# A graph layer in one launch: the second group of row sums, with ScalarE's high part ahead of the gate rows and an earlier reload of the partial sums

## The chip, the cores and the metric

The kernel runs on one core of a Trainium2 chip. The time is that of the device for one launch, in microseconds (us), and a kernel's time is the median of its runs.

## What is computed

The layer takes 1250 nodes with 1024 features and 20000 edges of 8 types. Cut to what matters here:

```python
xn = layernorm(x)
u = xn @ root + bias
for r in range(8):                       # relations
    mask = edge_type == r
    mean = segment_sum(xn[src] * mask, dst) / max(count, 1)
    u = u + mean @ weight[r]
z = concat([u, xn]) @ w_gate + b_gate
h = tanh(u) * z + xn * (1 - z)
x = x + h + linear_attention(xn)
x = x + fp4_ffn(layernorm(x))
```

## The kernel before, in words

The rows are cut into 10 tiles of 128 (NT). All products of the normalised x stand in one long run of TensorE: 21 column blocks (NH), each with 10 tiles, so 210 steps (NSTEP). Block 0 is the query, key and value projection, blocks 1 to 16 the eight relations with two halves each, 17 and 18 the root matrix, 19 and 20 the lower half of the gate matrix (from step 190, NT * H_GATE). Numbers are carried as a high part and a low part, so a step (`product`, L1877) is 24 matmuls of 128x512: high by high, high by low and low by high.

`xn[src] @ weight[r]` is taken as a product of all rows first; its results go to HBM (relation_rows), and the sums over edges are made by fetching rows of it. That is done in two groups of relations (0 to 4, then 5 to 7), tile by tile of the destination rows. For one tile of group two there are 7 items (`gather_items`, L133): places 0 and 3 are *left-over* items, places 1, 2, 4, 5 and 6 are *planes*. Ten tiles are spread over steps 178 to 207, so a tile takes three steps:

- step A: places 0, 1, 2; step B: places 3 and 4; step C: places 5 and 6.

Group two has the sums numbered 10 to 19 (`m.sum`). Each item is one fetched block of 128 rows of 1024 numbers, in a ring of 4 buffers (source_rows). GpSimd fetches item m + 4 as soon as item m has been used (`gather`, L940), with an indirect DMA.

A plane is one instruction of VectorE (`plane`, L1592, recorded at L1605): sum = rows * weight + sum, in u_sum0 or u_sum1 by the sum's parity. The first plane of a tile in group two reads the partial sum of group one, which SyncE has loaded back from HBM (`load_sum`, L696, recorded at L699).

A left-over item goes to TensorE. ScalarE makes its high part (`left_over_hi`, L2400, source_rows_hi, L2405), VectorE the one-hot (L1586) and the low part (`left_over`, L1583, source_rows_lo, L1589), and TensorE multiplies both by the one-hot at the end of the *next* step (`aggregate`, L2019, L2015, 4 matmuls). High and low part have one buffer each, so the next left-over item waits for these matmuls. After the low part of place 0 VectorE finishes the tile before (`finish`, L1609): it adds the matmuls' result (L1615) and the root rows (L1620), and SyncE stores the sum (`store_sum`, L701, L703) and loads the next root rows (`load_root`, L688, L694).

From step 190 on, VectorE empties a product's bank itself, since it adds the gate's bias (`evacuate_gate`, L1640, L1647), first thing in the step after the product. ScalarE only sends those rows out, with a DMA it issues after waiting for VectorE (`evacuate`, L2329, L2335). Before step 190 ScalarE empties the bank (L2345) and sends (L2347).

Each engine goes through the steps in its own program order:

- ScalarE (L2426): `evacuate(n - 1)`, `hi_row` (the high part of one 128x512 block of the weights to come, WH, L2317), `left_over_hi`;
- VectorE (L1652): `evacuate_gate(n - 1)`, then the step's items;
- GpSimd (L964): `low_rows` (L875, the low part WL of that block, L879), then the fetches;
- SyncE (L727): the load of the weight block four ahead (`load_raw`, L633, L642), which waits until an earlier block's low part is made, then for the items of the step: at place 2 `store_sum` and `load_root`, at place 5 `load_sum` for the next sum, which waits until the sum two before, from the same buffer, is stored (`stored_sum`, L518).

Of the kernel before, what the change touches and what calls it, by code (L numbers as in the profile page):

```python
# [22 lines left out]
NT = -(-N // P)  # L23
# [16 lines left out]
NBK = NG * NT  # L40
# [29 lines left out]
H_GATE = H_ROOT + 2  # L70
# [96 lines left out]
def gps_layer(nc, x, src, dst, edge_type_8, weight, root, bias, w_gate, b_gate, gamma, w_q, w_kv,  # L167
              w_out, ff_gate, ff_up, ff_down, out):
    with ExitStack() as ctx:
# [313 lines left out]
        def prod_bank(n):  # L483
            return 4 + n % 4
# [133 lines left out]
        def _(sp):  # L618
# [77 lines left out]
            def load_sum(rd, i):  # L696

                stored_sum(sp, rd, i - 2)
                sp.dma_start(ACCS[i % 2][:], u_d[rows(i % NT), :]).then_inc(sum_in[i % 2], 16)  # L699

            def store_sum(rd, i):  # L701
                sp.wait_ge(acc_done, NBK * rd + i + 1 + START)
                sp.dma_start(u_d[rows(i % NT), :], ACCS[i % 2][:]).then_inc(acc_out[i % 2], 16)  # L703
# [23 lines left out]
            for n in range(NSTEP + 1):  # L727
                h, t = n // NT, n % NT
                while raw_next < KT * min(h + 1, NH) + min(t, KT) + 4 and raw_next < KT * (NH + 1) + 4:
                    load_raw(raw_next)  # L730
                    raw_next += 1
                i, odd = divmod(n + 4 - KEYS_FROM, 2)
                if 0 <= i < NT and not odd:
                    load_qkv(i)
                i, odd = divmod(n + 4 - QUERIES_FROM, QUERIES_EACH)
                if 0 <= i < NT and not odd:
                    load_qkv(NT + i)
                if n == NT * H_GATE - 4:
                    sp.wait_ge(wq_out, 48 * R)
                    sp.dma_start(ZBIAS[:], b_gate.unsqueeze(0).broadcast_to([P, D])).then_inc(bgate_in, 16)  # L740
                if n == AGG_FROM[0] - 1:
                    sp.wait_ge(rounds_ready, 1)
                    sp.dma_start(BIASB[:], bias.unsqueeze(0).broadcast_to([P, D])).then_inc(bias_in, 16)
                for m in ITEMS_AT[n]:
                    if m.place == 2 and m.sum > 0:
                        store_sum(0, m.sum - 1)
                        if m.group == NG - 1:
                            load_root(m.sum)
                    if m.place == 5 and NT <= m.sum + 1 < NBK:
                        load_sum(0, m.sum + 1)  # L750

                if n == NSTEP - 6:
                    sp.wait_ge(prod, NSTEP - NT + 2)
                    load_u(1, 0)
                    load_u(1, 1)
                if n == NSTEP - 4:
                    sp.wait_ge(prod, NSTEP - NT + 4)
                    load_rows(0)
                    load_rows(1)
                if n == NSTEP - 2:  # L760
                    sp.wait_ge(prod, NSTEP - NT + 6)
                    load_gate_rows(0)
                    load_gate_rows(1)
                if n == NSTEP:
                    sp.wait_ge(prod, NSTEP - NT + 8)
                    load_mix_rows(0)
                    load_mix_rows(1)
# [1531 lines left out]
        def _(act):  # L2299
# [29 lines left out]
            def evacuate(n):  # L2329

                h, t, s = n // NT, n % NT, n % 4
                w = w_cols(h)
                if h >= H_GATE:
                    act.wait_ge(ev, n + 1)
                    act.dma_start(ev_home(n), ev_slot(s)).then_inc(ev_out[s], 16)  # L2335
                    return
                act.wait_ge(prod, n + 1)
                need(act, ev_out[s], 16 * (n // 4))
                if n == 0:
                    act.wait_ge(xt_ps, 2)  # L2340
                if h == 0:
                    a.activation(ev_slot(s)[:, 0:w], ps[:, prod_bank(n), 0:w], ACT.Copy,
                                 scale=qkv_scale[:, t:t + 1]).then_inc(ev, 1)
                else:
                    a.activation(ev_slot(s), ps[:, prod_bank(n), :], ACT.Copy).then_inc(ev, 1)  # L2345
                act.wait_ge(ev, n + 1)
                act.dma_start(ev_home(n), ev_slot(s)[:, 0:w]).then_inc(ev_out[s], 16)  # L2347
# [52 lines left out]
            def left_over_hi(m):  # L2400

                slot = m.index % RING
                act.wait_ge(xg_in[slot], 16 * (m.index // RING + 1))
                act.wait_ge(agg_used, FIRST + m.count)
                a.activation(OHI[:], XG[:, slot, :].bitcast(F32), ACT.Copy,  # L2405
                             scale=weight_list[:, m.column:m.column + 1]).then_inc(oh_hi, 1)
# [18 lines left out]
            norm_x(2)  # L2425
            for n in range(NSTEP):  # L2426
                h, t = n // NT, n % NT
                if n >= 1:
                    evacuate(n - 1)
                if 1 <= n < NT - 1:  # L2430
                    hi_x(n + 1)
                if 1 <= n < NT - 2:
                    norm_x(n + 2)
                ti, at = divmod(n - QUERIES_FROM, QUERIES_EACH)
                if n == KEYS_FROM + 2 * NT:
                    key_sums()
                    query_high(0)
                if 1 <= ti <= NT and at == 0:
                    copy_attention(ti - 1)
                    store_mix(ti - 1)  # L2440
                if 1 <= t <= KT and n < NSTEP:
                    hi_row(KT * (h + 1) + t - 1)
                if 0 <= ti < NT and at == 0:
                    copy_queries(ti)
                if 0 <= ti < NT - 1 and at == 1:
                    query_high(ti + 1)
                if n == AGG_FROM[0] - 1:
                    for s in range(2):
                        act.wait_ge(mix_out[s], 16 * NT // 2)
                for m in ITEMS_AT[n]:  # L2450
                    if m.place == 0 and m.tile == 0:
                        act.wait_ge(weights_in[m.group], 16 * NT * OVER[m.group])
                    if m.over:
                        left_over_hi(m)
                r, at = divmod(n - QUANT_FROM, QUANT_STEPS)
                if 0 <= r < R and at == 0:
                    if r == 0:
                        act.wait_ge(rounds_ready, 1)
                    else:
                        act.wait_ge(wq_out, 48 * r)  # L2460
                    for m in range(3):
                        act.dma_start(WQI[:, m, :], wf_flat[m][:, QU * r:QU * r + QU]).then_inc(wq_in, 16)
                if 0 <= r < R and at == 6:
                    act.wait_ge(wq_done, 3 * r + 3)
                    for m in range(3):
                        act.dma_start(wq_d[m][:, QU * r:QU * r + QU], WQI[:, m, :]).then_inc(wq_out, 16)
# [148 lines left out]
```

## Time and profile before

| | |
|---|---|
| median of 3 runs | 1571.64 us (1569.24 to 1573.2) |
| the profiled execution | 1573.55 us, its span 1571.8 us, 1.75 us around it |
| TensorE (PE) busy | 1529.8 us, 97% of the span, mean granted clock 0.998 |
| VectorE (DVE), GpSimd (POOL), ScalarE (ACT) busy | 891.7, 808.3, 412.0 us |
| DMA | 262.48 MB, mean 167 GB/s |

In the rows below a line of a timeline is: start in us, duration in us, engine, line, operation, out<-in, and in brackets the idle time of that engine before it and what ended it. An engine name with a q (SPq, ACTq) is its DMA issue.

### The profile page before, as it was taken

What the parts mean: (1) busy time and instruction counts of PE and PEld (TensorE: products, weight loads), DVE (VectorE), ACT (ScalarE), POOL (GpSimd) and SP (SyncE); (2) the same over time, 40 slices, a digit from 0 to 9 for tenths busy, and PEclk for the clock granted to TensorE, in tenths of its full rate; (3) what the DMA queues carried; (4) which work ended last, traced back from release to release, by engine and by line L of the source; (5) the groups of instructions that cost most, each with busy time, mean ns of one, the idle gap of its engine ahead of it and who ended that gap; (6) DMA issues with size and microseconds to landing.
All of it is one profiled execution on the core that took longest, in us unless ns stands there. A gap on an engine that the chain in (4) does not pass through costs nothing.

```text
span 1571.8 us, 19072 instructions
## 1 busy us (share of the span) xinstructions
PE 1529.8 (97%) x7138; PEld 1251.1 (80%) x7138; DVE 891.7 (57%) x1330; ACT 412.0 (26%) x598; POOL 808.3 (51%) x700
## 2 busy tenths in 40 slices
PE   6999999999999999999999999999998989999998
PEld 6987777777778688888888888888777767888897
DVE  5353222444442410005788888885567774798985
ACT  5421112222222112222222222322212113334230
POOL 5327766667664136567545545555656544342330
PEclk9999999999999999999999999999999999999999
DMA  6322333333333123238777777777889885452111
GB/s 227 109 101 77 83 90 91 109 103 117 104 96 114 64 83 100 81 104 289 246 235 258 244 257 265 259 263 238 290 307 313 294 311 209 174 181 61 41 41 51
DMA packets 120571, 262.48 MB, mean 167 GB/s; under 512 B 23465, under 2 KB 37024, under 8 KB 120472
## 3 DMA queue, kind: packets, MB, share of 16 engines
q1 hardware_dynamic: 48680, 109.34, 20.9%
q0 software_dynamic: 33056, 83.02, 17.5%
q10 hardware_dynamic: 38736, 68.83, 11.8%
q8 instruction: 58, 0.95, 0.2%
q14 instruction: 41, 0.34, 0.1%
HBM read 193.33 MB, written 80.06 MB: 174 GB/s over the span
## 4 chain that ended last, share of the span: by engine, by line
PE 72%; DVE 13%; issue 5%; DMA 5%; ACT 2%; POOL 2%; ACTq 0%; SPq 0%; DVEq 0%; POOLq 0%
PE ps L1888 57%; PE ps L2129 3%; DMA u_sum<-u_rows 3%; PE ps L2178 2%; PE ps L2015 2%; DMA source_rows<-relation_rows,row_list 2%; DVE u_sum L1605 2%; PE ps L2138 1%; PE ps L1971 1%; PE ps L2007 1%; PE ps L2218 1%; DVE source_rows_lo L1589 1%; ACT source_rows_hi L2405 1%; DVE U L1736 1%; PE ps L1995 1%
## 5 line engine op out<-in xcount | busy, mean ns | idle before, releaser
L1888 PE MATMUL ps<-WH,XTH 128*128 128x512 f32 (+1 forms) x1680 | 664.8, 396 | 0.5 <-DVE XTL L1100 0.5
L1888 PE MATMUL ps<-WH,XTL 128*128 128x512 f32 (+1 forms) x1680 | 651.2, 388 | 0.0
L1888 PE MATMUL ps<-WL,XTH 128*128 128x512 f32 (+1 forms) x1680 | 650.5, 387 | 0.0
L1888 PEld LDWEIGHTS ps<-WH,XTH 128*128 128x128 f32 x1680 | 316.5, 188 | 66.9 <-issue 7.1
L1888 PEld LDWEIGHTS ps<-WH,XTL 128*128 128x128 f32 x1680 | 315.5, 188 | 64.4
L879 POOL TENSOR_TENSOR WL<-RAW,WH 128x512 fp32r<-128x512 f32 x176 | 234.0, 1331 | 257.5 <-ACT WH L2317 255.2
L1888 PEld LDWEIGHTS ps<-WL,XTH 128*128 128x128 f32 x1680 | 316.1, 188 | 60.2 <-issue 2.4
L935 POOL DMA_INDIRECT source_rows<-relation_rows,row_list x180 | 218.1, 1212 | 244.4 <-DVE u_sum L1605 128.6
L2345 ACT ACTIVATE EV<-ps 128x512 f32<-128x512 f32 x180 | 107.5, 597 | 644.3 <-PE ps L1888 562.8
L956 POOL DMA_INDIRECT edge_lists<-edge_words x160 | 196.6, 1229 | 46.5 <-issue 45.0
L1605 DVE SCALAR_TENSOR_TENSOR u_sum<-source_rows,weight_list,u_sum 128x1024 f32<-128x1024 f32 x120 | 168.2, 1401 | 46.6 <-DMA source_rows<-relation_rows,row_list 31.6
L1589 DVE SCALAR_TENSOR_TENSOR source_rows_lo<-source_rows,weight_list,source_rows_hi 128x1024 fp32r<-128x1024 f32 x50 | 81.2, 1625 | 198.5 <-ACT source_rows_hi L2405 198.5
L2317 ACT ACTIVATE WH<-RAW 128x512 fp32r<-128x512 f32 x176 | 110.7, 632 | 150.2 <-DVE EV L1647 83.0
L2405 ACT ACTIVATE source_rows_hi<-source_rows,weight_list 128x1024 fp32r<-128x1024 f32 x50 | 57.3, 1146 | 100.3 <-DMA source_rows<-relation_rows,row_list 59.4
L1552 DVE TENSOR_TENSOR prefix<-ps,qkv_tile 128x544 f32<-128x544 f32 x40 | 29.0, 725 | 94.1 <-PE ps L1995 88.2
L2129 PE MATMUL ps<-WH,TH 128*128 128x512 f32 x160 | 63.1, 394 | 0.4 <-ACT TH L2495 0.4
L2129 PE MATMUL ps<-WL,TH 128*128 128x512 f32 x160 | 62.3, 389 | 0.0
L928 POOL DMA_INDIRECT weight_list<-edge_weights,weight_at x50 | 51.1, 1022 | 15.3 <-issue 9.6
L1045 POOL TENSOR_TENSOR xf<-xf,edge_words 128x1024 f32<-128x1024 f32 x10 | 20.3, 2034 | 68.8 <-DVE xf L1766 68.8
L1511 DVE COPY values<-qkv_tile 128x128 f32<-128x128 f32 x10 | 2.3, 233 | 93.1 <-PE ps L1975 82.3
L2015 PE MATMUL ps<-source_rows_hi,edge_one_hots 128*128 128x512 f32 x100 | 32.1, 402 | 16.5 <-DVE source_rows_lo L1589 16.4
L1554 DVE TENSOR_REDUCE prefix<-prefix 128x34 f32<-128x544 f32 x40 | 45.3, 1132 | 1.4
(330 smaller groups left out, 1504.0 us busy)
## 6 DMA issues: line engine op xcount, KB each, us to landing
relation_rows<-EV ACTq DMA_DIRECT2D x160, 256.0 KB
RAW<-in_L_gnn_weight SPq DMA_DIRECT2D x128, 256.0 KB
u_rows<-u_sum SPq DMA_DIRECT2D x20, 512.0 KB
RAW<-in_L_gnn_w_gate SPq DMA_DIRECT2D x32, 256.0 KB
mix_rows<-mix_rows_out ACTq DMA_DIRECT2D x10, 512.0 KB, 2.8
root_rows<-EV ACTq DMA_DIRECT2D x20, 256.0 KB
u_sum<-u_rows SPq DMA_DIRECT2D x10, 512.0 KB, 6.8
bias_rows<-root_rows SPq DMA_DIRECT2D x10, 512.0 KB
```

The costliest lines, as they stand in the source:

```text
L879: g.tensor_tensor(WL[:, h % 2, k, 0:w], RAW[:, q % 4, 0:w], WH[:, h % 2, k, 0:w].bitcast(F32), ALU.subtract).then_inc(w_lo, 1)
L928: return g.indirect_dma_start(out=weight_list[:, to:to + 1], out_offset=None, in_=rc_d, in_offset=bass.IndirectOffsetOnAxis(ap=places[:, a ...
L935: return g.indirect_dma_start(out=XG[:, slot, :].bitcast(F32), out_offset=None, in_=y_d[group], in_offset=bass.IndirectOffsetOnAxis(ap=row ...
L956: g.indirect_dma_start(out=list_d[k], out_offset=bass.IndirectOffsetOnAxis(ap=ew[0:EP, SLOT, c:c + 1].bitcast(U32), axis=0), in_=ew[0:EP, ...
L1589: v.scalar_tensor_tensor(OLO[:], XG[:, m.index % RING, :].bitcast(F32), weight_list[:, m.column:m.column + 1], OHI[:].bitcast(F32), ALU.mu ...
L1605: v.scalar_tensor_tensor(acc[:], XG[:, m.index % RING, :].bitcast(F32), weight_list[:, m.column:m.column + 1], base[:], ALU.mult, ALU.add) ...
L1888: mm = t_.matmul(ps[:, bank, 0:w], a[:, t, k, :], b[:, s, k, 0:w], start=(k == 0 and j == 0), stop=(k == KT - 1 and j == 2))
L2015: mm = t_.matmul(ps[:, bank + b, :], S1H[:, one_hot, :], part[:, 512 * b:512 * b + 512], start=(first and j == 0), stop=(last and j == 1))
L2129: t_.matmul(ps[:, 4 + 2 * s + b, :], TH[:, s, k, :], w[:, h % 2, k, :], start=(k == 0 and j == 0), stop=False)
L2317: a.activation(WH[:, h % 2, k, 0:w], raw(q), ACT.Copy).then_inc(w_hi, 1)
L2345: a.activation(ev_slot(s), ps[:, prod_bank(n), :], ACT.Copy).then_inc(ev, 1)
L2405: a.activation(OHI[:], XG[:, slot, :].bitcast(F32), ACT.Copy, scale=weight_list[:, m.column:m.column + 1]).then_inc(oh_hi, 1)
```

## The change

Two things move, and nothing is added or taken away. In ScalarE's loop the sending of the gate rows, steps 191 to 209, goes from the head of the step to behind `hi_row` and `left_over_hi`. In SyncE's loop the reload of the next partial sum goes from place 5 (step C) to place 3 (step B) in group two.

```diff
@@ SyncE's loop (L746) @@
                         if m.group == NG - 1:
                             load_root(m.sum)
-                    if m.place == 5 and NT <= m.sum + 1 < NBK:
+                    if m.place == (3 if m.group else 5) and NT <= m.sum + 1 < NBK:
                         load_sum(0, m.sum + 1)
@@ ScalarE's loop (L2426) @@
             for n in range(NSTEP):
                 h, t = n // NT, n % NT
-                if n >= 1:
+                if 1 <= n <= NT * H_GATE:
                     evacuate(n - 1)
...
                     if m.over:
                         left_over_hi(m)
+                if n > NT * H_GATE:
+                    evacuate(n - 1)
```

ScalarE, before, three steps (A, B, C) of one tile in the gate blocks; source_rows_hi is the high part of a left-over item, gate_x_rows<-EV the sending of gate rows:

```order
L2335 DMA gate_x_rows<-EV 128x512
L2317 ACTIVATE WH<-RAW 128x512
L2405 ACTIVATE source_rows_hi<-source_rows,weight_list 128x1024
L2335 DMA gate_x_rows<-EV 128x512
L2317 ACTIVATE WH<-RAW 128x512
L2405 ACTIVATE source_rows_hi<-source_rows,weight_list 128x1024
L2335 DMA gate_x_rows<-EV 128x512
L2317 ACTIVATE WH<-RAW 128x512
```

ScalarE with the change, the same three steps:

```order
L2317 ACTIVATE WH<-RAW 128x512
L2405 ACTIVATE source_rows_hi<-source_rows,weight_list 128x1024
L2335 DMA gate_x_rows<-EV 128x512
L2317 ACTIVATE WH<-RAW 128x512
L2405 ACTIVATE source_rows_hi<-source_rows,weight_list 128x1024
L2335 DMA gate_x_rows<-EV 128x512
L2317 ACTIVATE WH<-RAW 128x512
L2335 DMA gate_x_rows<-EV 128x512
```

The sending, and the wait for VectorE that stands before it, is now last in the step.

SyncE, before, from one store of a sum to the next (u_rows<-u_sum is the store, bias_rows the root rows, RAW a weight block, u_sum<-u_rows the reload):

```order
L703 DMA u_rows<-u_sum 128x1024
L694 DMA bias_rows<-root_rows 128x1024
L642 DMA RAW<-in_L_gnn_w_gate 128x512 x2
L699 DMA u_sum<-u_rows 128x1024
L642 DMA RAW<-in_L_gnn_w_gate 128x512
L703 DMA u_rows<-u_sum 128x1024
```

SyncE with the change:

```order
L703 DMA u_rows<-u_sum 128x1024
L694 DMA bias_rows<-root_rows 128x1024
L642 DMA RAW<-in_L_gnn_w_gate 128x512
L699 DMA u_sum<-u_rows 128x1024
L642 DMA RAW<-in_L_gnn_w_gate 128x512 x2
L703 DMA u_rows<-u_sum 128x1024
```

The reload now stands behind one weight block instead of two. TensorE, VectorE and GpSimd keep their orders.

## Rows read from the trace of the kernel before

**Rows 1.** The page, its first part: busy time of each engine and share

```profile
PE 1529.8 (97%) x7138; PEld 1251.1 (80%) x7138; DVE 891.7 (57%) x1330; ACT 412.0 (26%) x598; POOL 808.3 (51%) x700
```

**Rows 2.** Waits of TensorE from 1110 to 1290 us: total, times, longest

```profile
PE ps L2015 <- DVE source_rows_lo L1589: 16.4, 9, 3.1
```

**Rows 3.** Waits of TensorE from 1177 to 1286 us

```profile
PE ps L2015 <- DVE source_rows_lo L1589: 12.0, 6, 3.1
```

**Rows 4.** Timeline of TensorE

```profile
1161.30 0.50 PE L2015 MATMUL ps<-source_rows_hi,edge_one_hots 128*128 128x512 f32 x1 [1.78 <-DVE source_rows_lo L1589]
...
1182.52 0.50 PE L2015 MATMUL ps<-source_rows_hi,edge_one_hots 128*128 128x512 f32 x1 [2.76 <-DVE source_rows_lo L1589]
...
1264.29 0.74 PE L2015 MATMUL ps<-source_rows_hi,edge_one_hots 128*128 128x512 f32 x2 [3.10 <-DVE source_rows_lo L1589]
...
1265.33 0.39 PE L1888 MATMUL ps<-WH,XTH 128*128 128x512 f32 x1
...
1276.24 0.39 PE L2015 MATMUL ps<-source_rows_hi,edge_one_hots 128*128 128x512 f32 x1
```

**Rows 5.** Timeline of VectorE

```profile
1157.18 2.67 DVE L1605 SCALAR_TENSOR_TENSOR u_sum<-source_rows,weight_list,u_sum 128x1024 f32<-128x1024 f32 x2 [3.35 <-DMA u_sum<-u_rows]
...
1178.43 0.37 DVE L1586 TENSOR_SCALAR edge_one_hots<-iota,key_list 128x128 fp32r<-128x128 f16 x1
...
1241.36 1.29 DVE L1589 SCALAR_TENSOR_TENSOR source_rows_lo<-source_rows,weight_list,source_rows_hi 128x1024 fp32r<-128x1024 f32 x1 [1.35 <-ACT source_rows_hi L2405]
...
1262.44 1.79 DVE L1589 SCALAR_TENSOR_TENSOR source_rows_lo<-source_rows,weight_list,source_rows_hi 128x1024 fp32r<-128x1024 f32 x1 [1.87 <-ACT source_rows_hi L2405]
...
1271.59 3.04 DVE L1589 SCALAR_TENSOR_TENSOR source_rows_lo<-source_rows,weight_list,source_rows_hi 128x1024 fp32r<-128x1024 f32 x1 [1.74 <-ACT source_rows_hi L2405]
...
1280.12 0.38 DVE L1586 TENSOR_SCALAR edge_one_hots<-iota,key_list 128x128 fp32r<-128x128 f16 x1
1282.38 1.80 DVE L1589 SCALAR_TENSOR_TENSOR source_rows_lo<-source_rows,weight_list,source_rows_hi 128x1024 fp32r<-128x1024 f32 x1 [1.87 <-ACT source_rows_hi L2405]
```

**Rows 6.** Timeline of ScalarE

```profile
1157.96 1.16 ACT L2405 ACTIVATE source_rows_hi<-source_rows,weight_list 128x1024 fp32r<-128x1024 f32 x1 [7.16 <-DMA source_rows<-relation_rows,row_list]
...
1270.40 1.15 ACT L2405 ACTIVATE source_rows_hi<-source_rows,weight_list 128x1024 fp32r<-128x1024 f32 x1
...
1280.67 0.63 ACT L2317 ACTIVATE WH<-RAW 128x512 fp32r<-128x512 f32 x1 [9.11 <-DVE EV L1647]
1281.20 1.14 ACT L2405 ACTIVATE source_rows_hi<-source_rows,weight_list 128x1024 fp32r<-128x1024 f32 x1
```

**Rows 7.** Timeline of GpSimd

```profile
1148.02 0.99 POOL L935 DMA_INDIRECT source_rows<-relation_rows,row_list  x1 [0.30 <-issue]
...
1261.87 1.27 POOL L879 TENSOR_TENSOR WL<-RAW,WH 128x512 fp32r<-128x512 f32 x1
...
1265.00 1.30 POOL L935 DMA_INDIRECT source_rows<-relation_rows,row_list  x1 [1.86 <-DVE source_rows_lo L1589]
...
1272.24 1.30 POOL L879 TENSOR_TENSOR WL<-RAW,WH 128x512 fp32r<-128x512 f32 x1
```

**Rows 8.** Timeline of SyncE's DMA queue

```profile
1215.71 0.33 SPq L703 DMA_DIRECT2D u_rows<-u_sum  x1
...
1222.16 6.96 SPq L642 DMA_DIRECT2D RAW<-in_L_gnn_w_gate  x2
1229.16 0.48 SPq L699 DMA_DIRECT2D u_sum<-u_rows  x1
```

**Rows 9.** The chain that ended last, about 1164 us: a fetch beside a reload

```profile
1163.73 6.71 DMA source_rows<-relation_rows,row_list
```

**Rows 10.** The tile u_sum from 1080 to 1300 us: its reloads

```profile
DMA to landing us min/median/max: 6.0/6.8/10.2
```

**Rows 11.** Windows: length, busy PE, PEld, DVE, ACT, POOL, clock, DMA share, GB/s

```profile
1177.80:1279.50 101.70, 91.12 (x396) 73.61 (x395) 79.50 (x71) 19.20 (x23) 60.36 (x49) 1.00 0.90 306
...
1276.00:1290.00 14.00, 12.55 (x55) 10.04 (x54) 11.92 (x11) 2.31 (x3) 5.46 (x5) 1.00 0.99 369
```

## The prediction

> **What bounds the kernel now.** I read the page's first part, then TensorE's waits, then timelines of one tile. TensorE is busy 97% of the span, at full clock [rows 1, 11]: the kernel can gain only what TensorE idles, some 42 us in all. The stretch this change touches, group two, holds 16.4 us of it: nine waits of the left-over matmuls for VectorE's low part [rows 2]. Six of them, 12.0 us, lie in the gate blocks [rows 3], one per tile, always at place 3; the matmuls of place 0 start without a wait, as at 1276.24 [rows 4].
>
> What TensorE needs per tile: from 1265.33 to 1276.24, 10.91 us, it runs two products, so 5.455 us each; four left-over matmuls take about 0.92 us. Three products and two such sets make 18.2 us. It takes about 20.4 us, because a loop over VectorE, ScalarE and the fetches is longer. That loop has two legs, which I read in the tile around 1270 us.
>
> *Leg P*, low part of place 3 to low part of the next place 0. The low part ends at 1262.44 + 1.79 = 1264.23 [rows 5]; the fetch into that buffer starts at 1265.00 [rows 7], 0.8 later; ScalarE starts the high part at 1270.40 [rows 6], 5.4 after that; the low part runs from 1271.59 to 1274.63 [rows 5]. Together 10.40 us. The low part is 3.04 us long instead of 1.29 (as at 1241.36) because GpSimd's WL instruction, at 1272.24, falls into it [rows 7].
>
> *Leg Q*, low part of place 0 to low part of place 3: 1274.63 to 1282.38 + 1.80 = 1284.18, so 9.55 us. In it VectorE has the one-hot done at 1280.50 and then idles 1.87 us for ScalarE's high part [rows 5]. ScalarE was free for 9.11 us, waiting for VectorE to empty the gate bank, only to send those rows out; WH and the high part came behind that [rows 6]. The two engines wait for each other in turn. P + Q = 19.95 us here.
>
> **Part 1, ScalarE's order.** Nothing is added: the same sends, WH and high parts. The high part of place 3 now waits for its fetch and for the matmuls of place 0, which are done at about 1276.24 + 0.92 = 1277.2; it is made by 1278.4, and VectorE finds it ready at 1280.50. So 1.87 us go from Q. WL of step B also overlapped the low part (1.79 at 1262.44, with WL at 1261.87); started 1.87 earlier, at 1260.6, it ends when WL begins, and takes 1.29: another 0.5 us. Q becomes 9.55 - 1.87 - 0.5 = 7.2 us.
>
> P keeps its length from this part: at place 0 the high part comes on the landing of the fetch (1270.40), which neither the send nor WH delays by more than 0.2 us.
>
> The sends are late by up to one high part and its fetch's wait, some 2.4 us at step A. They are paid for by nobody as long as they land within the four steps (over 18 us) after which VectorE reuses that quarter of EV: cost 0.
>
> On the shared access of VectorE and GpSimd, row and rule say the same thing of why 1.29 becomes 3.04, but not of what follows. The Trainium skill ("SBUF — State Buffer", who interferes with whom) has it that a VectorE instruction with two SBUF inputs and a GpSimd instruction that reads SBUF exclude each other for a whole instruction, by order of issue. By that rule, should WL of step B come first by a hair, the low part would lose a whole WL and not the 0.5 us I take; that case is worked out from rows in rival B.
>
> **Part 2, the earlier reload.** In SyncE's queue it moves ahead of one weight block: from 1229.16 to right after the first of the two at 1222.16 [rows 8], some 6.6 us sooner. It landed 6.8 us after its issue in the median, 10.2 at most [rows 10], so it is there before the first plane in every tile but the first (whose reload waits for root rows, unchanged). What goes: in the gate blocks only small waits, already inside the six. In sum 13 VectorE waited 3.35 us [rows 5], but the high part of place 3 came at 1157.96 + 1.16 = 1159.12 anyway [rows 6] against the low part at about 1159.96: 0.8 us of the 1.78 [rows 4]. The reload now waits for the store of 1215.71; if that lands like the slowest reload, at 1226, SyncE is held, but the weight block behind it cannot go before 1228.8 (the end of the pair's wait), so nothing is late: cost 0.
>
> What it may cost: the reload now runs beside the fetch for place 0, which is in leg P. A fetch beside a reload took 6.71 us to the high part [rows 9]; without one 5.4. I add 1.3 to P; but the low part then starts 1.3 later and WL (1272.24 to 1273.54) is nearly out of its way, which gives back up to 1.1. P becomes 10.6 to 11.7. (The Trainium skill, "DMA: Bandwidth & Descriptors", issuing engines are not separate DMA queues, speaks against this part: whoever issues, all transfers interleave on the same 16 engines. By it the reload is no cheaper for standing in another engine's queue than the fetch; the 6.71 against 5.4 agrees.)
>
> **The sum.** P + Q = 17.8 to 18.9 us, against TensorE's 18.2. So TensorE sets the pace or misses it by up to 0.7 us per tile; I take 0.3. The first of the six is different: VectorE's one-hot ends at 1178.80 [rows 5], the low part at 1180.1, or 1180.6 beside a WL, and TensorE was ready at 1182.52 - 2.76 = 1179.76 [rows 4]; 0.7 us stay. Of the 12.0 us there remain 0.7 + 5 * 0.3 = 2.2, so 9.8 go, plus 0.8 in sum 13: 10.6, rounded to 10.5. All of group two lies ahead of the gate's second half on TensorE, whose work follows at once; what TensorE gains comes through to the end. Against the profiled execution: 1573.55 - 10.5 = 1563.05 us. That execution lies 1.9 above the median of the runs shown, so the forecast for the median is **1561.1 us**. Bounds of this case: 12.0 + 0.8 gained gives 1558.8; 0.7 left in every tile gives 12.0 - 4.2 + 0.8 = 8.6, so 1563.0.
>
> Can the DMA engines carry it? 306 GB/s over 101.7 us and five tiles [rows 11] is 6.2 MB per tile; in 18.2 us that is 342 GB/s. The 14 us from 1276 moved 369 at a share of 0.99, so yes, with little to spare.
>
> **The rivals.**
>
> *A (0.50): as forecast*, 1558.5 to 1564.
>
> *B (0.22): the loop stays longer than TensorE's need.* Either DMA at 0.90 share scales no further (306 / 0.90 = 340 GB/s, 18.3 us per tile, and gaps on top), or WL of step B comes first and costs the low part a WL (1.3 us) in place of 0.5. With a tile of 19.1 us, 0.9 idle in each, 12.0 - 5.4 + 0.8 = 7.4 less to 5 less: 1564 to 1567. For it: the DMA share is already high. Against: the highest share in a tile's length was reached with more GB/s, not fewer.
>
> *C (0.20): the wait moves to the fetch.* The fetch for place 0 takes about 8 us: P = 10.4 + 2.6 = 13.0, P + Q = 20.2, as before. 0 to 5 us gained: 1566.9 to 1572. It is also the case in which the change does not do what it says, because the high part never was what VectorE waited for but its fetch; at place 0 this is so already, at place 3 rows 5 and 6 speak against it.
>
> *D (0.08): slower.* Reload and fetch for place 0 hold each other up as in the worst fetch of the stretch: issued at 1148.02 beside a reload and one more transfer of that size, its high part began at 1157.96, 9.9 us later [rows 6, 7]. With it P = 10.4 + 4.5 = 14.9, P + Q = 22.1, so 1.7 us more per tile than 20.4, for five tiles 8.5 less 0.8: 1579. It decides from a fetch of about 8.3 us up. Against it: the extra transfer there was a single one.
>
> **How the numbers follow.** A measurement of this kernel can tell about 0.3%, 4.7 us, from no change: below 1566.9 is faster, above 1576.4 slower. A and B are faster (0.72); C gives no change (0.20); D is slower (0.08). The range from 1557.5 to 1570 holds A and B and half of C and leaves 0.2 outside.
>
> **What the profile will show.** If right: the wait of source_rows_lo for source_rows_hi at place 3 is gone (those at place 0, which are the fetch's, stay), TensorE's waits for source_rows_lo from steps 190 on fall from 12.0 to about 2 us, tiles come every 18.2 to 18.6 us, and the DMA rate in this stretch rises to about 340 GB/s. The reloads are issued between the two weight blocks, and no plane waits for one after the first. It is wrong if TensorE's waits keep more than 5 us, if high parts start more than 8 us after their fetches, if WL sits inside the low part of place 3, or if a new idle time shows behind 1285 us that takes back what group two gave.

## The result and the profile after

| | before | after |
|---|---|---|
| median | 1573.06 us (1569.24 to 1581.23, 22 runs) | 1567.86 us (1564.04 to 1570.9, 22 runs) |
| ratio, 95% interval | | 0.9963 (0.9953 to 0.9972) |
| the profiled execution | 1573.55 us, span 1571.8 | 1568.32 us, span 1566.5 |

The change makes the kernel faster by 0.37%, some 5.8 us: half of the 10.5 forecast. Profile against profile it is 5.2 us. The median lies 6.8 us above the forecast of 1561.1: 5.3 of them are the missing gain, profile against profile, and 1.4 come from the median of before, 1573.06 over 22 runs and not the 1571.64 of three that the forecast started from.

The page's first part, against [rows 1]: no work has gone, TensorE's share is a point higher.

```profile
PE 1532.2 (98%) x7138; PEld 1253.7 (80%) x7138; DVE 881.9 (56%) x1330; ACT 412.5 (26%) x598; POOL 810.9 (52%) x700
```

TensorE's waits from 1110 to 1290 us and from 1177 to 1286 us, against [rows 2, 3] (total, times, longest), then its waits behind 1290 us:

```profile
PE ps L2015 <- DVE source_rows_lo L1589: 7.5, 12, 1.5
...
PE ps L2015 <- DVE source_rows_lo L1589: 6.2, 10, 1.5
...
PE ps L2113 <- issue: 3.2, 1, 3.2
```

16.4 us have become 7.5, but in more pieces: each tile now has a short wait at place 3 and a longer one at place 0. In TensorE's timeline, against [rows 4], the rows at 1157.36 and 1176.94 are place 3; those at 1209.28 and 1229.73, which had no wait before, are place 0. The last two rows are the last matmul of the products and the transposes behind it, the first work after group two.

```profile
1157.36 0.62 PE L2015 MATMUL ps<-source_rows_hi,edge_one_hots 128*128 128x512 f32 x2
...
1176.94 0.73 PE L2015 MATMUL ps<-source_rows_hi,edge_one_hots 128*128 128x512 f32 x2 [0.24 <-DVE source_rows_lo L1589]
...
1209.28 0.70 PE L2015 MATMUL ps<-source_rows_hi,edge_one_hots 128*128 128x512 f32 x2 [1.20 <-DVE source_rows_lo L1589]
...
1229.73 0.70 PE L2015 MATMUL ps<-source_rows_hi,edge_one_hots 128*128 128x512 f32 x2 [1.46 <-DVE source_rows_lo L1589]
...
1288.37 0.39 PE L1888 MATMUL ps<-WH,XTL 128*128 128x512 f32 x1
...
1291.98 3.62 PE L2113 MATMUL ps<-ident,u_tile 128*128 128x128 f32 x16 [3.22 <-issue]
```

The same last two in the timeline of before, where the transposes waited 1.21 us and not 3.22:

```profile
1295.95 0.39 PE L1888 MATMUL ps<-WH,XTL 128*128 128x512 f32 x1
1297.55 1.96 PE L2113 MATMUL ps<-ident,u_tile 128*128 128x128 f32 x16 [1.21 <-issue]
```

So one can say where TensorE stands against before at four points:

| the same instruction | before | after | ahead |
|---|---|---|---|
| place 3 of the last tile ahead of the gate blocks | 1161.30 [rows 4] | 1157.36 | 3.9 us |
| last matmul of the products | 1295.95 | 1288.37 | 7.6 us |
| first transposes behind them | 1297.55 | 1291.98 | 5.6 us |
| end of the span | 1571.8 | 1566.5 | 5.3 us |

3.9 us come ahead of the gate blocks, 3.6 within them, and 2.3 are lost behind them. The sum had 0.8, 9.8 and none. Of the 3.6, 1.6 come up to the first place 3 of the gate blocks (1182.52 before, 1176.94 after) and 2.0 in the five tiles behind it.

**The gate blocks.** Windows from one place-3 set to the next, three of the five (length, busy PE, PEld, DVE, ACT, POOL, clock, DMA share, GB/s):

```profile
1176.94:1195.97 19.03, 18.71 (x80) 14.86 (x80) 14.24 (x15) 4.09 (x5) 13.13 (x11) 1.00 0.96 337
...
1216.16:1236.96 20.80, 18.75 (x80) 14.86 (x80) 14.23 (x15) 2.94 (x3) 12.38 (x10) 1.00 0.84 296
...
1256.82:1276.65 19.83, 18.75 (x80) 14.86 (x80) 13.90 (x15) 4.09 (x5) 13.63 (x11) 1.00 0.97 340
```

Five tiles take 99.7 us, 19.94 each, where they took 20.34 (101.7 us from the first of [rows 4] at place 3, 1182.52, to the last, 1284.23). One tile in the timelines of VectorE, ScalarE, GpSimd and SyncE's queue:

```profile
1214.82 1.28 DVE L1589 SCALAR_TENSOR_TENSOR source_rows_lo<-source_rows,weight_list,source_rows_hi 128x1024 fp32r<-128x1024 f32 x1
...
1220.09 3.52 DVE L1605 SCALAR_TENSOR_TENSOR u_sum<-source_rows,weight_list,u_sum 128x1024 f32<-128x1024 f32 x2 [2.20 <-DMA source_rows<-relation_rows,row_list]
...
1228.30 1.28 DVE L1589 SCALAR_TENSOR_TENSOR source_rows_lo<-source_rows,weight_list,source_rows_hi 128x1024 fp32r<-128x1024 f32 x1 [3.78 <-ACT source_rows_hi L2405]
```

```profile
1227.12 1.15 ACT L2405 ACTIVATE source_rows_hi<-source_rows,weight_list 128x1024 fp32r<-128x1024 f32 x1 [11.31 <-DMA source_rows<-relation_rows,row_list]
```

```profile
1216.99 1.46 POOL L879 TENSOR_TENSOR WL<-RAW,WH 128x512 fp32r<-128x512 f32 x1
1218.61 1.01 POOL L935 DMA_INDIRECT source_rows<-relation_rows,row_list  x1 [0.15 <-issue]
```

```profile
1218.48 0.33 SPq L642 DMA_DIRECT2D RAW<-in_L_gnn_w_gate  x1
1218.86 0.45 SPq L699 DMA_DIRECT2D u_sum<-u_rows  x1
```

At 1214.82 the low part of place 3 starts without a wait, and takes 1.28: the wait of 1.87 in [rows 5] is gone. At 1228.30 the low part of place 0 has waited 3.78, against 1.74 before, and ScalarE's high part says for what: its fetch. That fetch starts at 1218.61, 2.5 us behind the low part's end at 1216.10 and not 0.8. WL of step B stands in front of it in GpSimd's queue, as it did before; but there it was over at 1263.14, before the low part ended at 1264.23 [rows 5, 7], and here it runs from 1216.99 to 1218.45. 0.25 us after it the reload is issued. The high part begins 8.5 us after the fetch's start, the longest of the five; the mean is 7.5.

### The profile page after: what moved, and what is told of

Same layout as the page of the kernel before. It is cut to its first block, busy times and chain, and to the rows that moved or that the text cites. A ratio compares the mean times of both kernels' runs of the same rounds, so it can differ in the third digit from the quotient of the medians.

```text
span 1566.5 us, 19072 instructions
## 1 busy us (share of the span) xinstructions
PE 1532.2 (98%) x7138; PEld 1253.7 (80%) x7138; DVE 881.9 (56%) x1330; ACT 412.5 (26%) x598; POOL 810.9 (52%) x700
## 4 chain that ended last, share of the span: by engine, by line
PE 77%; DVE 10%; issue 5%; DMA 5%; POOL 2%; ACT 1%; SPq 0%; POOLq 0%; DVEq 0%; ACTq 0%
PE ps L1888 61%; DMA source_rows<-relation_rows,row_list 4%; PE ps L2129 3%; PE ps L2178 2%; PE ps L2015 2%; PE ps L2138 1%; PE ps L1971 1%; PE ps L2007 1%; PE ps L2218 1%; POOL source_rows L935 1%; PE ps L1995 1%; DVE u_sum L1605 1%; DVE EV L1731 1%; ACT source_rows_hi L2405 1%; DVE u_sum L1615 1%
## 5 line engine op out<-in xcount | busy, mean ns | idle before, releaser
L1605 DVE SCALAR_TENSOR_TENSOR u_sum<-source_rows,weight_list,u_sum 128x1024 f32<-128x1024 f32 x120 | 173.7, 1448 | 50.3 <-DMA source_rows<-relation_rows,row_list 43.2
L1589 DVE SCALAR_TENSOR_TENSOR source_rows_lo<-source_rows,weight_list,source_rows_hi 128x1024 fp32r<-128x1024 f32 x50 | 71.1, 1421 | 193.9 <-ACT source_rows_hi L2405 190.7
L2138 PE MATMUL ps<-WH,TL 128*128 128x512 f32 x160 | 39.6, 390 | 0.0
```

What stands on the lines that cost most here:

```text
L1589: v.scalar_tensor_tensor(OLO[:], XG[:, m.index % RING, :].bitcast(F32), weight_list[:, m.column:m.column + 1], OHI[:].bitcast(F32), ALU.mu ...
L1605: v.scalar_tensor_tensor(acc[:], XG[:, m.index % RING, :].bitcast(F32), weight_list[:, m.column:m.column + 1], base[:], ALU.mult, ALU.add) ...
L2138: mm = t_.matmul(ps[:, 4 + 2 * s + b, :], TL[:, s, k, :], WH[:, h % 2, k, :], start=False, stop=(k == KT - 1))
```

## The experiments

All kernels were compared with the kernel before. *Start* is from the end of the low part of place 3 to the start of the fetch for place 0, *fetch* from there to the start of its high part, *rest* from there to the low part's end; these make leg P. Each is a mean over five tiles of the gate blocks, read from the timelines, and so is leg Q, over the five that follow these. Before, one tile gave 10.4 and 9.55 in the prediction; the means are in the first line. TensorE alone needs 18.2 us for P + Q. Each line is one profiled execution; before and after, taken once more, gave 5.5 and 7.4 us for the fetch.

| kernel | ratio (95%) | start | fetch | rest | P | Q |
|---|---|---|---|---|---|---|
| before | 1 | 1.0 | 5.7 | 3.6 | 10.4 | 10.0 |
| reload only | 0.9982 (0.9971 to 0.9993) | 1.0 | 6.8 | 2.9 | 10.7 | 9.4 |
| ScalarE only | 0.9991 (0.9975 to 1.0007) | 2.2 | 6.1 | 3.0 | 11.3 | 8.9 |
| after, both | 0.9963 (0.9953 to 0.9972) | 2.4 | 7.5 | 2.9 | 12.9 | 7.1 |
| fetches first | 0.9982 (0.9970 to 0.9994) | 1.3 | 6.5 | 3.7 | 11.4 | 8.2 |
| fetches first, old reload | 0.9994 (0.9975 to 1.0013) | 1.3 | 6.2 | 3.5 | 10.9 | 9.1 |
| no WL | 0.9962 (0.9947 to 0.9976) | 1.4 | 8.5 | 2.5 | 12.3 | 7.0 |
| no root rows | 0.9951 (0.9930 to 0.9973) | 2.4 | 7.5 | 2.7 | 12.6 | 7.0 |
| no reload | 0.9933 (0.9910 to 0.9956) | 2.4 | 6.4 | 2.8 | 11.6 | 7.7 |
| neither | 0.9898 (0.9862 to 0.9934) | 2.4 | 5.8 | 3.7 | 11.9 | 7.1 |

### The two parts alone

ScalarE's new order, with the reload at place 5 in both groups:

```diff
-                    if m.place == (3 if m.group else 5) and NT <= m.sum + 1 < NBK:
+                    if m.place == 5 and NT <= m.sum + 1 < NBK:
```

> The change's ScalarE part alone; the reload of the partial sums stays at place 5. Theory T (the gain of leg Q is given back in leg P, because GpSimd's WL of step B now stands in front of the fetch for place 0, and because that fetch takes longer with the reload beside it): leg Q is about 7 to 8 us as in the changed kernel, the fetch for place 0 still starts some 2.5 us after the low part of place 3, but takes nearer 5.4 to 6.5 us than the 7.5 of the changed kernel; VectorE waits for late reloads in leg Q instead. 3 to 6 us less than before. Rival R (the transfers as a whole set the pace, whichever order they are issued in): tiles of 19.9 us as in the changed kernel, 5 to 6 us less, the fetch still at about 7.5. Rival S (the gain of the change came from the reload): within 2 us of before.

It took 1569.47 us against 1571.67; the interval of its ratio takes in 1, so this part alone is not shown to gain. Two of the five Q come to 7.3 us; the others are longer, because first planes now wait for the late reload (up to 1.4 us), and one low part met two WL back to back (timelines of VectorE and GpSimd):

```profile
1271.99 4.20 DVE L1589 SCALAR_TENSOR_TENSOR source_rows_lo<-source_rows,weight_list,source_rows_hi 128x1024 fp32r<-128x1024 f32 x1 [0.37 <-ACT source_rows_hi L2405]
```

```profile
1272.61 2.48 POOL L879 TENSOR_TENSOR WL<-RAW,WH 128x512 fp32r<-128x512 f32 x2
```

With 1.3 us in place of these 4.2 the mean Q would be 8.3. TensorE waited 4.9 us behind it, its longest wait for a low part in any of these profiles.

The reload at place 3, with ScalarE's old order:

```diff
-                if 1 <= n <= NT * H_GATE:
+                if n >= 1:
                     evacuate(n - 1)
...
-                if n > NT * H_GATE:
-                    evacuate(n - 1)
```

> The change's reload part alone; ScalarE keeps its order. Theory T: VectorE keeps its waits of 1.87 us for the high part at place 3, its waits for reloads go (3.35 us in sum 13, 0.3 to 1.8 after), the fetch for place 0 starts 0.8 us after the low part of place 3 and takes 6 to 7 us because the reload is beside it: 0 to 3 us less than before. Rival S: 5 to 6 us less, as the whole change. A fetch that still takes 5.4 us would clear the reload of the longer fetch in the changed kernel.

It took 1570.37 us against 1571.67. The start is as before, the fetch 1.1 us longer: the reload beside it costs that, against the 1.3 of the sum. Q keeps its wait. By their ratios the parts alone gain 1.4 and 2.8 us, together 4.2; with their intervals that agrees with the 5.8 of both.

### GpSimd's order: is WL in front of the fetch the loss?

In step B, WL goes behind the two fetches; the rest is as after.

```diff
+                late = n >= AGG_FROM[1] and any(m.place == 0 for m in GATHERS_AT[n])
-                if 1 <= t <= KT and 4 < n < NSTEP:
+                if 1 <= t <= KT and 4 < n < NSTEP and not late:
                     low_rows(KT * (h + 1) + t - 1)
...
                 for m in GATHERS_AT[n]:
                     gather(m)
+                if 1 <= t <= KT and 4 < n < NSTEP and late:
+                    low_rows(KT * (h + 1) + t - 1)
```

> The changed kernel, and in GpSimd's loop, in step B of group two alone, WL stands behind the two fetches instead of in front of them. Theory T: the fetch for place 0 starts 0.8 us after the low part of place 3 instead of 2.5; leg P falls from 12.9 to 11.2 to 11.7, tiles from 19.9 to 18.3 to 18.9 us, TensorE's waits for the low part from 6.2 to 1 to 3 us; 4 to 7 us less than the changed kernel, so 9 to 13 less than before. Rival R: the fetch starts earlier but takes as much longer; tiles stay at 19.5 to 20 us and the time within 2 us of the changed kernel.

1569.32 us against 1571.67, so no better than after. The fetch starts 1.1 us sooner and lands sooner, but WL comes back elsewhere: in the tile shown above two planes, 2.7 us by themselves, run beside two WL (timeline of VectorE).

```profile
1221.54 5.38 DVE L1608 SCALAR_TENSOR_TENSOR u_sum<-source_rows,weight_list,u_sum 128x1024 f32<-128x1024 f32 x2 [0.83 <-DMA source_rows<-relation_rows,row_list]
```

P falls by 1.5 us and Q rises by 1.1, so P + Q is 19.6 and not 19.9. The time also holds a loss that P + Q does not show: ahead of the gate blocks TensorE waited 3.40 us, and its granted clock fell behind that (last section). The same with the reload back at place 5:

> The kernel with ScalarE's new order, but the reload back at place 5, and GpSimd's WL of step B behind the two fetches. It brings together the short fetch start (+0.8 instead of +2.5 us) and a fetch for place 0 with no reload beside it. If bytes in flight set the landing (the theory the runs so far favour): the fetch takes 5.6 to 6.4 us as with ScalarE's part alone, leg P comes to 9 to 11 us, but leg Q stays over 8 us, because the first plane waits for the late reload and the planes run beside two WL; tiles of 19.5 to 20 us, 1567 to 1570 us, no better than the changed kernel. If the fetch's start is what counts (WL in front of it), P + Q falls to TensorE's 18.2 us and the time to about 1562 us.

1571.17 us against 1573.48. P is the shortest of any kernel with the new order of ScalarE, Q about as long as with ScalarE's part alone (planes wait 3.1 us for reloads); P + Q is 20.0. No gain is measured, though its profile too holds two waits, of 3.48 and 3.72 us, with a lower clock behind them.

WL of the steps 190 to 209 left out altogether (so the low part of these weights is not made):

```diff
                 pool.wait_ge(w_hi, q + 1)
+                if KT * (H_GATE + 1) <= q < KT * (H_UP + 0) + KT:
+                    pool.sem_inc(w_lo, 1)
+                    return
```

> The changed kernel without GpSimd's WL instructions of steps 190 to 209: it raises the semaphore alone, so the low parts of the last two blocks of weights are missing from the result. Theory T: the fetch for place 0 starts 0.8 us after the low part of place 3 instead of 2.5, no VectorE instruction is lengthened by WL; leg P falls from 12.9 to about 11.0 us, P + Q to 18.0, and TensorE sets the pace: waits for the low part from steps 190 on at 0 to 2 us, tiles of 18.3 to 18.8 us, 5 to 8 us less than the changed kernel. Rival R (the transfers set the pace): tiles stay at 19.3 to 20 us, 0 to 3 us less.

1567.63 us against 1574.26: the ratio of after. The fetch starts 1.1 us sooner than after and lands at the same time: start and fetch are 9.8 us together, after 9.9. Timelines of GpSimd and ScalarE in the tile of 1216:

```profile
1218.32 0.99 POOL L938 DMA_INDIRECT source_rows<-relation_rows,row_list  x1 [0.30 <-issue]
```

```profile
1226.87 1.15 ACT L2408 ACTIVATE source_rows_hi<-source_rows,weight_list 128x1024 fp32r<-128x1024 f32 x1 [9.99 <-DMA source_rows<-relation_rows,row_list]
```

Once WL is out of the way, the planes wait for fetches instead: 27.3 us of such waits from 1177 to 1286 us, 11.7 after. P + Q is 19.3, 0.6 less than after, where 1.7 would bring it to TensorE's 18.2. So taking WL away gives back about a third of what is missing; the rest stays, in fetches that take 8.5 us here and not 7.5. (Why they do was not tried.)

### Bytes: is it the load on the DMA engines?

The reloads of sums 12 to 19 left out (these sums lack group one's part):

```diff
-                sp.dma_start(ACCS[i % 2][:], u_d[rows(i % NT), :]).then_inc(sum_in[i % 2], 16)
+                if isinstance(rd, int) and rd == 0 and i > NT + 1:
+                    sp.sem_inc(sum_in[i % 2], 16)
+                else:
+                    sp.dma_start(ACCS[i % 2][:], u_d[rows(i % NT), :]).then_inc(sum_in[i % 2], 16)
```

> The changed kernel without the reloads of the sums 12 to 19: SyncE waits as before and raises the semaphore itself, so the first group's partial sums of these tiles are missing from the result. 4.2 MB less are moved in the stretch. Theory T: the fetch for place 0 still starts 2.5 us after the low part of place 3, and its 7.5 us fall to 5.5 to 6.5; tiles of 18.7 to 19.3 us, 3 to 6 us less than the changed kernel. Rival R: tiles fall by the reload's share of the bytes, 0.5 of 6.2 MB, 8%, to 18.3 us, and the fetch falls below 5.5. If the fetch stays at 7.5, the reload has nothing to do with it.

1561.93 us against 1571.67. The fetch takes 6.4 us, 1.1 less than after: the reload's price again, here with ScalarE's new order.

A transfer of the same size, but some 7 us ahead of the fetch: the root rows (L694) of sums 12 to 19 left out in the same way, so these sums lack them.

> The changed kernel without the loads of the root rows for the sums 12 to 19 (SyncE raises the semaphore itself, so stale rows are added to these sums): 512 KB less per tile, as in the run without reloads (10.5 us less than before, against 5.8 of the changed kernel), but issued behind the store in step A, some 7 us before the fetch for place 0 and the reload. Theory R (in steps A to B the DMA engines are a queue that is full, and the fetch for place 0 lands when what was issued before it has moved, whatever it is): about the same gain as without reloads, 3 to 6 us less than the changed kernel, the fetch for place 0 at 6.3 to 7 us instead of 7.6. Rival N (only the transfer next to the fetch counts): within 1.5 us of the changed kernel, the fetch stays at 7.5.

1567.63 us against 1575.71. The fetch takes 7.5 us, as after, and the ratio's interval takes in that of after. So with the reload in place the fetch is held by what is issued beside it, and not by this earlier transfer. (The Trainium skill, "DMA: Bandwidth & Descriptors", issuing engines are not separate DMA queues, has all transfers interleave on the same 16 engines. The run without the reload agrees: SyncE's transfer cost GpSimd's fetch 1.1 us.)

Both left out:

> The changed kernel with neither the reloads nor the root rows of the sums 12 to 19: 1 MB of the 6.2 MB of a tile is gone. Theory R: leg P falls to 10 to 11 us, P + Q below 18.2, TensorE sets the pace; its waits for the low part from steps 190 on are under 2 us, and the time is 8 to 11 us less than the changed kernel, 14 to 17 less than before, less what the hole behind the last product takes. Rival N: no more than without reloads alone.

1559.95 us against 1575.71, some 10 us less than after by the ratios. Here the rival by which only the near transfer counts fails, as the full queue failed in the run before: the fetch is 5.8 us and not the 6.4 without reloads alone, and TensorE's waits from 1110 to 1290 us are 1.8 us and not 4.0. So the root rows cost nothing that can be measured while the reload is there, and 0.6 us of fetch once it is gone; the two prices do not simply add, and why is open. Now TensorE all but sets the pace. Its waits from 1110 to 1290 us, and a window over five tiles:

```profile
PE ps L2021 <- DVE source_rows_lo L1595: 1.8, 5, 0.7
```

```profile
1170.00:1270.00 100.00, 98.31 (x426) 79.18 (x425) 83.84 (x77) 21.09 (x25) 68.42 (x50) 1.00 0.86 274
```

TensorE idles 1.7 of 100 us, and its five tiles take 18.9 us each. That is near case A of the prediction, which had 18.2 to 18.6; it takes 1 MB less per tile to get there.

### The load that after has in bursts

The DMA share of four-microsecond windows of after, over one fetch for place 0 and behind it:

```profile
1220.00:1224.00 4.00, 4.00 (x19) 3.33 (x18) 3.80 (x3) 0.00 (x0) 3.83 (x3) 1.00 0.95 306
1224.00:1228.00 4.00, 4.00 (x19) 3.19 (x17) 0.53 (x2) 0.88 (x1) 1.50 (x2) 1.00 1.00 385
1228.00:1232.00 4.00, 2.54 (x12) 1.91 (x11) 3.66 (x4) 0.65 (x2) 0.99 (x1) 1.00 0.36 140
```

All 16 engines are full until the fetch lands, and two thirds idle while the loop turns to the next. The buffers of the ring come free in bunches, so fetches go out in bunches.

### What is lost behind the products

Before the first transposes TensorE stands still for 3.22 us, before 1.21, with no releaser in the profile. The loads of the rows of tiles 0 and 1 start at that time, so they were put behind the transposes, first in after, then in before:

```diff
-                if n == NSTEP - 2:
-                    sp.wait_ge(prod, NSTEP - NT + 6)
-                    load_gate_rows(0)
-                    load_gate_rows(1)
...
+            sp.wait_ge(ut_ps, 1)
+            for t in range(2):
+                load_gate_rows(t)
+            for t in range(2):
+                load_mix_rows(t)
```

> The changed kernel, with SyncE's four loads of gate and mix rows for the tiles 0 and 1 (2 MB) issued only after TensorE's first transposes of the next stage. The question is the hole behind the last product: TensorE waits 3.2 us there in the changed kernel and 1.2 before, and its first 16 transposes take 3.6 us instead of 2.0, with the granted clock at 0.57 in that stretch. Theory H (TensorE's instructions for the next stage come late, because these loads fill the DMA engines just then): the hole falls to about 1.2 us and the transposes to 2.0, so 2 to 4 us less than the changed kernel, 8 to 10 less than before. Rival I (it is the instruction fetch or a register load with a fixed price, or ScalarE's new order, and has nothing to do with the loads): the hole stays at 3 us or more, the time within 1.5 us of the changed kernel, or slower where the late loads hold up the next stage.

> The same late loads in the kernel before, whose hole is 1.2 us. Theory H: nothing to gain, within 1.5 us of before. If this one gains as much as the changed kernel does from them, the loads cost something else than the hole. If it is slower by 2 us or more, the late loads hold up the next stage, and that price stands in the changed kernel's run too.

After with late loads took 1569.52 us against 1574.26 (0.9974, 0.9959 to 0.9989), before with them 1575.79 (1.0008, 0.9993 to 1.0022). The hole was 1.99 us in the first and 2.87 in the second, where it stood at half a DMA load (windows):

```profile
1296.00:1299.00 3.00, 0.39 (x2) 0.00 (x0) 0.69 (x1) 0.00 (x0) 0.00 (x0) 1.00 0.50 198
1299.00:1302.00 3.00, 2.73 (x17) 2.74 (x17) 0.25 (x1) 1.31 (x2) 0.00 (x0) 0.68 0.32 26
```

So the hole does not need full DMA engines, nor ScalarE's new order. Over all profiles it was 1.2 to 1.5 us in before (twice) and with the reload alone, 2.0 to 4.7 in the eleven others. What sets it stays open.

### The two kernels once more

> The changed kernel once more, for the hole behind TensorE's last product. If it is a property of the kernel it is again about 3.2 us, with transposes of 3.6 us behind it; if it belongs to the execution it comes out anywhere from 1.2 to 4.7 us, as over the other kernels.

> The kernel before once more. If the hole is a property of the kernel it is again 1.2 us, with transposes of 2.0 us; if it belongs to the execution it differs.

One execution each: 1569.98 and 1577.22 us. P of after is 12.7 and Q 7.0, but for one tile of 10.8, whose low part ran from 1274.4 beside WL and took 4.3 us. Before gives P 10.0, Q 10.8, and the hole 1.46. The hole of after is 3.09, so it is no accident of one run.

## Why the prediction was half right

The direction was right and the size wrong: 10.5 us forecast, 5.2 measured between the profiles. The median of 1567.86 us lies in rival C's bounds (1566.9 to 1572), and in the stated range of 1557.5 to 1570 only because that range took in half of C. Step by step:

**Leg Q, right.** Forecast 7.2 us, measured 7.1. The wait for ScalarE at place 3 is gone, and so is WL from the low part.

**"P keeps its length from this part", wrong.** This step failed. The sum had P at 10.6 to 11.7; it is 12.9, 2.5 us more than before. By its pieces: the start +1.4, the fetch +1.8, the rest -0.7. Each was there to be seen:

- The start. I let the low part of place 3 end when WL of step B begins, and left it there. But on GpSimd the fetch for place 0 stands behind WL in one queue, and waits for that low part as well. Once the low part ends before WL begins, it is WL that the fetch waits for. With ScalarE's part alone the start is 2.2 already; with WL behind the fetch, or left out, it is 1.3 and 1.4.
- The fetch. The reload beside it was priced right (1.3 forecast; 1.1 with the reload alone, 1.1 between after and no reload, 1.4 between after and ScalarE's part alone). Unpriced was that ScalarE's new order itself lengthens the fetch, by 0.4 (ScalarE only) to 0.7 us (no reload). The reason was not tried by itself, and one profile each is thin: the two of before are 0.2 apart.
- Taking the later start back gave little: with no WL at all the fetch lands at the same time and P + Q falls by 0.6 us, with WL behind the fetches P falls by 1.5 us and Q takes 1.1 back. So the landing is the term to look at first, not the start.

P + Q is then 19.9 and not 17.8 to 18.9, and the gate blocks gave 3.6 us for 9.8. (The one tile that the sum was read from was 0.4 us shorter than the mean of five, 19.95 against 20.35.) This is rival C's mechanism: the wait moves to the fetch (P 13.0 forecast, 12.9 measured; rival C had all of it in the fetch, and 1.4 are the start's). It had a chance of 0.20, and in the gate blocks it is what happened. That place 0 had no wait before [rows 4] was no sign of room: TensorE came late to it, because it had waited at place 3.

**The tiles ahead of the gate blocks, too small.** I gave sum 13 0.8 us and nothing to the two before. They gave 3.9, over half of what TensorE gained up to the last product, and the forecast has no credit for it. I had looked for waits of planes for their reload at one tile only; VectorE's timeline of before, then of after, shows another, in sum 11:

```profile
1116.96 2.67 DVE L1605 SCALAR_TENSOR_TENSOR u_sum<-source_rows,weight_list,u_sum 128x1024 f32<-128x1024 f32 x2 [3.08 <-DMA u_sum<-u_rows]
```

```profile
1114.46 2.67 DVE L1605 SCALAR_TENSOR_TENSOR u_sum<-source_rows,weight_list,u_sum 128x1024 f32<-128x1024 f32 x2 [0.46 <-DMA u_sum<-u_rows]
```

In the second profile of before these waits were smaller (1.5 us from 1100 to 1165 and not 6.4), and TensorE lost 2.9 us and not 4.3 there: the 3.9 is one execution's, and 2 to 4 is the size. How much of it is the reload's I can't say closer: with ScalarE's part alone, which changes nothing up to there, that profile had no wait of TensorE at the first two places either.

**"What TensorE gains comes through to the end", not quite.** 2.0 of the 7.6 us went in the longer hole, 0.3 behind it. The prediction named such an idle time behind 1285 us as a sign of being wrong, but gave it no price.

**No effect seen:** the sends going out later (nobody waits for EV), and SyncE's wait on the store (3.8 us, once). DMA carried 337 and 340 GB/s in two tiles, as the estimate asked, but 293 to 316 in the three others.

**Waits cost more than they list.** TensorE's waits fell by 8.9 us up to the last product, and it gained 7.6. The 18.2 us of a tile hold where there is no wait. In the five tiles from 1182.52 before, 101.7 us less 9.3 of listed waits, one to a tile, make 18.5 each; after, 99.7 less 6.0, two to a tile, 18.75. So each wait costs some 0.3 us beside itself, an estimate from these four numbers, and two half waits cost more than one whole, as long as the clock stays up.

**The four signs.** High part at place 3 ready: yes. TensorE's waits at about 2 us: no, 6.2. Tiles of 18.2 to 18.6 us: no, 19.9. WL inside the low part of place 3: no, as forecast; WL in front of the fetch was not on the list. Of its signs of being wrong, two came whole (TensorE's waits over 5 us, a new idle time behind 1285 us) and one in part: one high part of the five started more than 8 us after its fetch (8.5).

## What to carry to other kernels

In a loop of several engines a wait that is removed moves every instruction behind it, on all the queues of the loop. Follow each leg once round with the new times, the next instruction in each queue included, before giving the gain to the pacemaker; here the saved 2.9 us of one leg came back as 2.5 in the other. Where DMA engines are full in bursts, price a fetch by what is issued within a few microseconds of it and not by the mean GB/s: half a megabyte cost 1.1 us beside the fetch and nothing measurable 7 us ahead of it. But the far one is only hidden behind the near one: with the near one gone, it cost 0.6.

## What the runs showed of the hardware

**A fetch's time goes with what is beside it.** The same indirect fetch of 128 rows, from its start to the high part made of it, took 5.7 to 8.5 us in the mean of five tiles, over ten kernels that differ in the order and number of the other transfers and of WL.

**An instruction of VectorE can grow by whole instructions of GpSimd.** The low part takes 1.28 us alone, 3.04 beside one WL [rows 5, 7] and 4.20 beside two back to back, 2.48 us long. The Trainium skill ("SBUF — State Buffer", who interferes with whom) has an exclusive lock by order of issue; alone 1.3 and WL 2.5 give 3.8, so the row agrees but for 0.4. VectorE's instruction lost both WL though it had begun first, which the rule taken by the profile's starts would not give; starts on GpSimd are rough in the profile.

**A standstill of TensorE can be followed by its lower clock.** Windows of after, the first of them the standstill and the start of the transposes:

```profile
1288.00:1292.00 4.00, 0.78 (x5) 0.32 (x3) 0.69 (x1) 0.00 (x0) 0.00 (x0) 1.00 1.03 392
1292.00:1296.00 4.00, 4.00 (x19) 3.91 (x20) 0.59 (x1) 1.89 (x3) 0.17 (x1) 0.57 0.98 388
```

The same place before:

```profile
1297.00:1300.00 3.00, 2.06 (x17) 1.83 (x17) 0.07 (x1) 1.17 (x2) 0.00 (x0) 1.00 1.03 384
```

A granted clock of 0.57 is mostly the level of 1.2 GHz; 16 transposes took 3.62 us there and 1.96 at 2.4 GHz. There are 14 profiles. In the four with a standstill of 1.99 us or less the transposes took 1.96 us; in nine of the ten with 2.85 us or more they took 2.70 to 3.67, and in one, with 3.48, again 1.96. It cost little at the end: the slower transposes took 1.7 us more, and shorter waits behind them gave most of it back.

Within the loop it costs more, and the sums above do not have it. Fetches first (timeline of TensorE), from place 3 of the last tile ahead of the gate blocks to the next place 0:

```profile
1159.78 1.22 PE L2018 MATMUL ps<-source_rows_hi,edge_one_hots 128*128 128x512 f32 x2 [3.40 <-DVE source_rows_lo L1592]
...
1174.36 0.62 PE L2018 MATMUL ps<-source_rows_hi,edge_one_hots 128*128 128x512 f32 x2
```

That is 14.58 us, with no other wait in it and a granted clock of 0.81; before took 11.92 for the same (1161.30 to 1173.22), at 1.00. The 15 longest waits of TensorE for a low part, from 1110 to 1290 us of the 14 profiles, are 2.29 to 4.92 us. Behind ten of them the granted clock of the next 13 to 15 us was 0.79 to 0.88; in the eight that can be measured to the next place 0 it cost 1.5 to 2.8 us. Behind the five others (2.32, 2.76, 2.79 twice, 3.10) it stayed at 1.00, both long waits of the profiled before among them; before, taken once more, has two (2.80 and 2.54) and paid for both, 1.6 and 1.5. After has no wait over 1.5 us in its profile, and one of 4.0 when taken once more. In the 87 executions of before made beside the experiments the mean granted clock was 0.995 to 0.996 on each chip, in the 22 of after 0.997. So part of the 5.8 us may be clock that shorter waits kept up; how much, no run separates.
